# Scaling the probability tiles on ScalarE instead of VectorE in a fused attention and mixture-of-experts kernel

## The reference

```python
h = _layernorm(x) * (1 + ca) + sa
q = (h @ wq).reshape(b, s, H, NOPE + ROPE);  ckv = h @ wkv_a
...
scores = jnp.einsum('bqhd,bkhd->bhqk', qf, k) * scale
scores = jnp.where(causal[None, None], scores, jnp.float32(-1e+30))
attn = jax.nn.softmax(scores, axis=-1)
o = jnp.einsum('bhqk,bkhd->bqhd', attn, v).reshape(b, s, H * VD)
x = x + ga * (o @ wo)
h = _layernorm(x) * (1 + cb) + sb
routed = jnp.einsum('bsed,bse->bsd', _experts_all(h, rg, rgb, rw1, rb1, rw2, rb2), combine)
x = x + gb * (h + shared + routed)
```

## Time and profile before

| | |
|---|---|
| median of 3 runs | 1533.46 us (1527.58 to 1537.03) |
| profiled execution | 1530.34 us, its span 1528.7 us |
| TensorE busy | 1372.6 us (90% of the span) |
| VectorE busy | 941.5 us (62%) |
| ScalarE busy | 560.6 us (37%) |
| GpSimd busy | 395.7 us (26%) |
| line 1138, the scaling | 256 instructions, 113.6 us busy |
| granted TensorE clock, mean | 0.96 |

### The profile page before, as it was taken

One profiled execution on the slowest core, in us unless ns is written; L12 is line 12 of the kernel. 1 busy time (PEld: TensorE's weight loads), 2 busy tenths in 40 slices (PEclk: granted clock), 3 DMA queues, 4 the chain that ended last, 5 costly groups with the idle time before them and its releaser, 6 DMA issues. The chain is left out here.

```text
span 1528.7 us, 23824 instructions
## 1 busy us (share of the span) xinstructions
PE 1372.6 (90%) x7108; PEld 1158.0 (76%) x7108; DVE 941.5 (62%) x1993; ACT 560.6 (37%) x1279; POOL 395.7 (26%) x314
## 2 busy tenths in 40 slices
PE   6848887599999998999989999998799899998994
PEld 3436775488888887888878888887687688787873
DVE  2456774377677778767796777875554343343438
ACT  2322222254445444444444544443321232232222
POOL 0002666200000318003090030820827000000035
PEclk9968999799999999999999999999899999999997
DMA  9976898799989756877679966682748778888357
GB/s 337 403 250 173 240 302 268 240 331 332 308 285 333 235 196 227 285 271 247 216 270 359 312 216 217 202 311 81 283 146 314 266 260 314 298 326 311 134 190 257
DMA packets 179955, 403.13 MB, mean 264 GB/s; under 512 B 24557, under 2 KB 81841, under 8 KB 169637
## 3 DMA queue, kind: packets, MB, share of 16 engines
q1 hardware_dynamic: 160968, 299.62, 58.1%
q0 software_dynamic: 18912, 102.57, 17.9%
HBM read 250.56 MB, written 151.57 MB: 263 GB/s over the span
## 5 line engine op out<-in xcount | busy, mean ns | idle before, releaser
L1067 ACT ACTIVATE a_pr<-a_pr,a_nmax 128x128 f32<-128x128 f32 (+3 forms) x256 | 142.2, 556 | 118.4 <-DVE a_nmax L1130 118.2
L1230 PE MATMUL a_psY<-a_pT,a_cv 128*128 128x256 f32 (+2 forms) x768 | 135.2, 326 | 1.9 <-DVE a_pT L1152 1.9
L1230 PEld LDWEIGHTS a_psY<-a_pT,a_cv 128*128 128x128 f32 x768 | 125.8, 190 | 14.6 <-issue 2.1
L1130 DVE CUSTOM_DVE_ANT_0 a_pr<-a_psS,a_mask 128x128 f32<-128x128 f32 (+3 forms) x256 | 115.3, 486 | 33.2 <-PE a_psS L1218 32.4
L102 PE MATMUL a_psX<-a_hT,a_wqk 128*128 128x512 f32 (+1 forms) x256 | 100.7, 393 | 22.0 <-DMA a_wqk<-wqk_d 22.0
L1138 DVE TENSOR_SCALAR a_pr<-a_pr,a_rinv 128x128 f32<-128x128 f32 (+3 forms) x256 | 113.6, 508 | 2.2
L1163 DVE TENSOR_TENSOR n_acc<-a_psZ,n_acc 128x512 f32<-128x512 f32 x125 | 86.2, 689 | 35.3 <-PE a_psZ L104 33.4
L1147 DVE TENSOR_TENSOR a_oT<-a_psY,a_oT 128x512 fp32r<-128x512 f32 x64 | 44.1, 689 | 96.8 <-ACT a_oT L1078 96.8
L104 PE MATMUL a_psX<-a_hT,a_wqk 128*128 128x512 f32 (+1 forms) x256 | 100.6, 393 | 0.0
L103 PE MATMUL a_psX<-a_hT,a_wqk 128*128 128x512 f32 (+1 forms) x256 | 100.5, 393 | 0.0
L102 PE MATMUL a_psZ<-a_mh,a_oT 128*128 128x512 f32 x250 | 98.2, 393 | 0.8 <-issue 0.8
(11 more groups left out here) (291 smaller groups left out, 3499.7 us busy)
## 6 DMA issues: line engine op xcount, KB each, us to landing
w1s_d<-a_ws SPq DMA_DIRECT2D x72, 512.0 KB, 2.9
a_wqk<-wqk_d SPq DMA_DIRECT2D x64, 512.0 KB, 4.9
a_mh<-mhl_d SPq DMA_DIRECT2D x32, 1024.0 KB, 6.5
s_ring<-w1s_d POOLq DMA_DIRECT2D x13, 2048.0 KB, 9.2
w2s_d<-a_ws SPq DMA_DIRECT2D x72, 256.0 KB, 3.4
qpe_d<-p_qs SPq DMA_DIRECT2D x64, 256.0 KB, 4.3
a_qpe<-qpe_d SPq DMA_DIRECT2D x64, 256.0 KB, 3.9
a_rw<-in_L_ffn_rw SPq DMA_DIRECT2D x128, 128.0 KB, 3.6
```

Of the source, the lines that this page charges most:

```text
L1067: nc.scalar.activation(pr[i], pr[i], ACT.Exp, bias=nmax[:, i:i + 1], scale=-1.0, accum_out=rsum[:, i:i + 1]).then_inc(ex, 1)
L1130: nc.vector.tensor_tensor_reduce(out=pr[i], in0=score[i][:, 0:w], in1=mask[:, S - w:S], scale=-1.0, scalar=3e38, op0=ALU.add, op1=ALU.min, ...
L1230: m = nc.tensor.matmul(psY[:, q0:S], cv[:, j, cs], pT[:, ps, o:o + w], start=n == 0, stop=n == 11)
```

## The change

The four multiplications by the reciprocal leave VectorE's stream and become four copies with a per-row scale on ScalarE, in place, behind `split_high` of the head's first chunk and ahead of `q_high`. The reciprocal stays on VectorE; ScalarE waits for it (`rc`). `nr`, for which the transposes wait, is now counted up by ScalarE.

```diff
+                def shares(g):
+                    act.wait_ge(rc, g + 1)
+                    for i in range(TB):
+                        nc.scalar.activation(pr[i], pr[i], ACT.Copy, scale=rinv[:, i:i + 1]).then_inc(nr, 1)
+
...
                         exps(g)
                         split_high(*todo[0])
+                        shares(g)
                         if not (last and u):
                             q_high(g + 1)
...
                     nc.vector.reciprocal(rinv[:, :], rsum[:, :]).then_inc(rc, 1)
-                    dve.wait_ge(rc, g + 1)
-                    for i in range(TB):
-                        nc.vector.tensor_scalar(pr[i], pr[i], rinv[:, i:i + 1], None, ALU.mult).then_inc(nr, 1)
```

## The result

| | before | after |
|---|---|---|
| median | 1531.87 us (4 runs, 1527.58 to 1537.03) | 1506.52 us (4 runs, 1503.61 to 1511.73) |
| ratio | | 0.984 (95% interval 0.982 to 0.987) |
| profiled execution, span | 1528.7 us | 1503.5 us |
| VectorE busy | 941.5 us | 829.7 us |
| ScalarE busy | 560.6 us | 667.4 us |

The changed kernel is 1.6% faster. Of the 25.2 us between the two spans, 22.4 lie between the start of head 0 and the start of head 63 (758.0 us before, 735.7 after: 286.25 to 1044.29, and 285.71 to 1021.40).

A forecast was written before the change was run, and what follows sets the result against it. TensorE, busy 90% of the span, was taken as the bound, its waits for VectorE as the recoverable time. Terms -15.6 - 7.5 + 3.1 = -20.0 us gave 1510.3 on the profiled execution, 1513 as median; range 1505 to 1525.

The forecast's parts named there:

- Where the time was: Heads over 11.69 us each: 26.9 us excess together, mostly GpSimd slowing VectorE's scaling; a late DMA chunk in head 44.
- The disturbed heads: Heads 19, 25 to 27, 57, 58 and two like 19: waits vanish with scaling on ScalarE, gaining 15.6 us.
- The price of the scaling: Four scaled copies on ScalarE take 1.93 us, read from the exps' rows, against 1.28 on VectorE.
- The ordinary head: Transposes keep 1.4 us of slack behind the query's low part, so ordinary heads cost nothing.
- The opening: Heads 0 to 2, where transposes start right behind L1142: +1.0 us each, +3.1 in all, bounds +2 to +6.
- the prediction's signs: For the opening: three waits of the transposes for L1142, about 1 to 3 us, in heads 0 to 2.
- Heads 40 to 47: Heads with two weight chunks each: 7.5 us gained of 11.3 at stake, bounds 4.5 and 11.3, limited by DMA queues.
- L1156 beside GpSimd: VectorE's instruction behind the scaling stays slowed, 2.0 us in GpSimd's stretches, with nobody waiting.
- The DMA: Rival, chance 0.19: heads 40 to 47 end with the transfers and gain nothing; -12.5 us, 1521.
- GpSimd does not slow ScalarE's copies: Rival claimed the opposite, chance 0.06: scaling takes 5.4 us on ScalarE too, 1537 us.
- ScalarE's chain: Rival, chance 0.05: four copies over 3.3 us make all ordinary heads wait; at 4.0 us, 1555 us.
- The sum: Whole kernel: -15.6 - 7.5 + 3.1 = -20.0 us, to 1513; this forecast's chance 0.70.

## Why the prediction was right, and where its sizes were off

- **Where the time was.** Predicted: only the heads over 11.69 us can give anything back, and their cause, in all but 44 and 45, is GpSimd beside VectorE's scaling. Shown by the trace after, and by the two runs that took away either the fast form or GpSimd's compute, for nine heads: 19, 25, 26, 35, 41, 42, 51, 57 and 58. Heads 27 and 43 the prediction read wrongly: their scaling took the ordinary 1.27 us, and the 1.5 and 1.2 us over 11.69 came with a lowered clock behind the waits ahead of them.
- **The disturbed heads,** -15.6 us for heads 19, 25 to 27, 35, 51, 57 and 58, and -6.5 for 41 to 43: all of them at 11.69 us after, clock 1.00: both terms as forecast.
- **The price of the scaling,** 1.93 us from the exps' rows: 1.91. The exps were the right neighbour; the shapes took 388, 494, 601 and 708 ns.
- **The ordinary head.** 1.4 us of slack forecast, up to the transposes' first matmul; by that measure 1.7 (8.96 to 10.69 us into a head), and 1.6 by their first weight load, which the run with twice the scaling bears out. No ordinary head grew.
- **The opening,** +3.1 us forecast, +2.2 measured (31.71 against 29.50, clocks 0.95 and 0.94). At full clock it takes 30.21 us in the change timed again, about 10.07 us a head, against 9.32 a head scaled on VectorE: 0.75 us a head instead of 1.0. TensorE's waits for L1145 in it were three, as the prediction's signs said, 4.6 us in all and 2.8 at most. I had put the split, the four copies and the query copy end to end; each starts about 0.1 us before the one ahead of it ends (the scaling at 592.21, the split's end at 592.31), and I had used that overlap only among the four.
- **Heads 40 to 47,** the term that was mis-sized: -7.5 forecast, and -6.5 - 2.4 = -8.9 measured in heads 41 to 45. I had feared that the transfers would take more back, from rates of 335 and 358 GB/s. In heads 44 and 45 they ran at 387 GB/s. The mechanism was there: a chunk 3.80 us late in head 45, with the scaling queued behind it. The prediction puts GpSimd's loads in the same queues as the chunks; the profile has them in two queues over the same 16 DMA engines (q0 moved 2.1 MB from 808 to 826 us in the kernel before, which are GpSimd's two loads, and q1 4.7 MB).
- **L1156 beside GpSimd** (now L1159), 2.02 us forecast, 1.50 in head 26, where VectorE then waited 0.80 us for the query copy. It can be longer: 3.01 us in head 42, and there L1145 followed with no wait, 0.6 us later in the head than usual.

```profile
779.43 3.01 DVE L1159 TENSOR_TENSOR a_ws<-a_rw,a_ws 128x768 fp32r<-128x768 f32 x1 [0.32 <-ACT a_ws L1093]
782.36 0.68 DVE L1145 SCALAR_TENSOR_TENSOR a_qT<-a_psX,a_qT 128x512 fp32r<-128x512 f32 x1
```

- **The rivals.** The DMA took back 2.4 us of the 26.9, where the rival needed all 11.3 of heads 41 to 45. But the sign that the prediction named for this rival, more than 3 us of ScalarE idle for chunks in heads 42 to 46, did show: it was 8.2 us (1.9, 1.6, 3.8 and 1.0 in heads 42, 44, 45 and 46). The sign was ill chosen: of these 8.2 us TensorE waited for 2.1, and the slack took the rest. GpSimd does not slow ScalarE's copies: 1.91 us in heads 25 and 26 as elsewhere. ScalarE's chain is 1.91 us against a bound of 3.3; with twice the scaling it was 3.9, and the kernel was slower than before, 1551.26 us (one run) against 1533.14. By the slack of 1.6 us the bound in an ordinary head is 3.5.
- **The sum.** -20.0 us forecast; -15.6 - 8.9 + 2.2 = -22.3 in the attention. The spans of the two profiled executions differ by 25.2 us, 2.8 of it outside heads 0 to 62, in stages whose code did not change. The median of the first runs fell by 25.3, from 1531.87 and not from the 1533.46 that I had started with, and by 22.8 when the change was timed again; both agree with the traces' 22.4 and 24.0 as far as the runs' spread can tell. So 1506.5 is 6.5 us under 1513 and a little under the forecast's own 1508.5 to 1519.4; it is in the stated range because of the 4 us added for the runs' spread. Of the 6.5 us, 2.3 come from the terms, the rest from the stages around and from which executions the medians fell on.

## To carry to other kernels

A long instruction group on VectorE that works from SBUF to SBUF in its fast form should be looked up in the stretches where GpSimd computes: here its mean over the kernel (508 ns) hid a factor of 3 to 4 in nine of 64 heads. The remedy need not be another engine: the same instruction with an accumulator output costs 0.7 us more for the four tiles and kept its length beside GpSimd. Where work moves to another engine, its place in the row decides: it belongs where that engine waits anyway, and the other engine's stream behind it has to be read too.

## What I had not expected of the hardware

- The accumulating tensor_scalar kept its length beside GpSimd to within 5 ns (742 mean, 747 at most, for 512 columns), while the plain one went from 1.28 to 5.44 us for four and a two-input tensor_tensor next to it from 0.95 to between 1.05 and 2.05, once 3.01. GpSimd lost far less: its four steps of 128x512 took 5.19 us beside the slowed scaling of head 26, and 5.06 just ahead of it.
- The 16 DMA engines moved 387 GB/s over 25.8 us, and 405 over 17.8 us in the run without GpSimd's compute, at shares of 1.04 (the profile's own figure, over 1 as it stands); heads 44 and 45 of the kernel before had moved 358 at 1.00.
- The part from head 63 to the end, unchanged, took 479.0 to 487.7 us in single executions.
